# Differential attention on one core: the gate and up products of a feed-forward tile are issued together behind both head pairs' scores, and their tangent one step later

## What is computed

```python
xn = _layernorm(x)
# differential attention: 16 score maps (8 heads x 2), head size 8, causal
scores = jnp.einsum('bhqd,bhkd->bhqk', q, k)
attn = jax.nn.softmax(where(causal, scores, -inf), axis=-1)
attn = attn[:, :, 0] - lam * attn[:, :, 1]
out = jnp.einsum('bhqk,bhkd->bhqd', attn, v)
# feed-forward gate: 4-bit blockwise rounding of inputs and weights
gate = fp4_linear(xn, w_gate)        # 128 -> 352
y = fp4_linear(xn, w_up)             # 128 -> 352
g = _silu(fp4_linear(silu(gate) * y, w_down))   # 352 -> 128
x = x + s * g
```

## Time and profile before

| what | value |
|---|---|
| median of three runs | 691.15 us |
| profiled execution, span | 687.9 us |
| PE matmul busy in the span | 86% |
| ACT busy in the span | 72% |
| DVE busy in the span | 77% |
| one iteration of the middle loop | 40.56 us |

### The profile page before, as it was taken

The page is one execution under the profiler, slowest core; times in us unless marked ns, Lnnn a source line. Parts: engine busy times, 40 slices in busy tenths (PEclk is TensorE's granted clock), DMA queues, the critical chain, the costliest instruction groups (busy, mean ns, idle before and its releaser), DMA issues. The chain is left out here.

```text
span 687.9 us, 15892 instructions
## 1 busy us (share of the span) xinstructions
PE 590.2 (86%) x4825; PEld 355.3 (52%) x4826; DVE 530.8 (77%) x1425; ACT 496.5 (72%) x843; POOL 326.7 (47%) x466
## 2 busy tenths in 40 slices
PE   3576765899999999999999999977999799999960
PEld 2465554233333333333333333375877589999960
DVE  3999998687978889797888877779798856555575
ACT  2367795798989989898998999923455467777741
POOL 0224345344534344452434544252477777776661
PEclk9799998799999999999999999998899979999995
DMA  8000001000544566644466650041122233333475
GB/s 218 16 16 31 20 13 61 1 1 2 102 91 74 82 116 116 115 88 91 63 106 116 116 106 12 1 157 59 59 82 74 80 82 102 95 103 91 131 208 166
DMA packets 76265, 56.06 MB, mean 81 GB/s; under 512 B 6528, under 2 KB 70848, under 8 KB 75968
## 3 DMA queue, kind: packets, MB, share of 16 engines
q1 hardware_dynamic: 70688, 46.01, 30.8%
q0 software_dynamic: 4352, 8.99, 3.9%
q10 hardware_dynamic: 1184, 0.56, 0.3%
HBM read 15.36 MB, written 28.65 MB: 64 GB/s over the span
## 5 line engine op out<-in xcount | busy, mean ns | idle before, releaser
L787 ACT ACTIVATE attend_prob<-attend_ring 128x1024 f32<-128x1024 f32 (+1 forms) x320 | 280.0, 951 | 16.4 <-PE attend_ring L933 14.4
L731 POOL TENSOR_SCALAR_AFFINE_SELECT attend_prob<-attend_prob 128x256 f32<-128x256 f32 x256 | 118.0, 485 | 141.4 <-ACT attend_prob L787 140.8
L953 PE MATMUL attend_ps_o<-attend_prob,attend_v_slot 128*32 128x512 f32 (+3 forms) x1536 | 156.6, 496 | 0.0
L933 PE MATMUL attend_ring<-attend_qk_slot 32*128 32x512 f16 (+3 forms) x672 | 80.1, 329 | 8.1 <-ACT attend_prob L787 6.3
L1907 POOL DMA_INDIRECT expert_outputs<-routed_linear_gated,routed_expert_goal_now x72 | 70.3, 977 | 29.7 <-issue 23.9
L1033 POOL DMA_INDIRECT slots<-rows,slot_index x64 | 62.1, 971 | 37.3 <-issue 33.2
L933 PEld LDWEIGHTS attend_ring<-attend_qk_slot 32*128 32x128 f16 x672 | 22.4, 91 | 106.7 <-ACT attend_prob L787 37.6
L1935 DVE TENSOR_TENSOR outed_linear_head_normed<-outed_linear_head_normed,routed_linear_ps_c 128x256 f32<-128x256 f32 x72 | 30.2, 420 | 41.3 <-ACT outed_linear_head_normed L2029 36.8
L953 PEld LDWEIGHTS attend_ps_o<-attend_prob,attend_v_slot 128*32 128x32 f32 x1536 | 33.7, 108 | 44.9 <-issue 37.7
L2076 PE MATMUL routed_linear_ps_c<-outed_linear_head_normed,head_turned 128*128 128x128 f32 x384 | 52.5, 281 | 1.1 <-ACT head_turned L2010 1.1
L369 POOL TENSOR_TENSOR project_parts_q<-project_rotated_q,project_parts_q 128x1024 f16<-128x1024 f32 x8 | 17.6, 2201 | 68.9 <-ACT project_parts_q L417 68.9
(11 more groups left out here) (291 smaller groups left out, 1281.8 us busy)
## 6 DMA issues: line engine op xcount, KB each, us to landing
slots<-attend_zeros SPq DMA_DIRECT2D x24, 715.0 KB, 10.2
attend_qk_slot<-qk_parts SPq DMA_DIRECT2D x14, 512.0 KB, 3.1
x_pairs<-slots SPq DMA_DIRECT2D x72, 65.0 KB
v_all<-expert_outputs SPq DMA_DIRECT2D x8, 512.0 KB, 5.5
xn_all<-project_xn SPq DMA_DIRECT2D x8, 256.0 KB, 2.3
w<-w_laid SPq DMA_DIRECT2D x1, 2048.0 KB, 7.8
rows<-rows SPq DMA_DIRECT2D x4, 512.0 KB, 3.8
out<-xn_all SPq DMA_DIRECT2D x8, 256.0 KB, 3.5
```

Source lines behind the costliest of these rows:

```text
L731: ins = nc.gpsimd.affine_select(out=edge, in_=edge, compare_op=ALU.is_ge, fill=0.0, base=0, pattern=[[0, 2], [1, P]], channel_multiplier=-1)
L787: nc.scalar.activation(probs(k, pair)[:, :, 0:width], scores[:, :, 0:width], ACT.Exp, scale=HD ** -0.5).then_inc(exp_made[u][pair], 1)
L933: ins = nc.tensor.matmul(dst[:, s * QC + at:s * QC + at + cols], qk[rows, T + j * P:T + (j + 1) * P], qk[rows, qc * QC + off:(qc + 1) * QC ...
L953: ins = nc.tensor.matmul(ps_o[RB * s:RB * (s + 1), off:QC], v4[slot][:, j, s], probs(k, s // 2)[:, s % 2, at:at + cols], start=j == 0, sto ...
```

## The change

In `ORDER` and in PE's queue, the gate product of a tile moves from ahead of its step's scores to behind both pairs' scores, and the up product, which stood between the pairs, follows the gate product directly. The tangent on ACT moves from ahead of the exponentials of step 5i + 3 to behind them (`GATED` = 4). On DVE the two products move by 3 ticks, and the seven parts of the rounding by 3 ticks. Nothing is added or taken out; no shape changes.

```diff
-        GATE, HIDDEN, DOWN, CHUNK = 3, 7, 9, 11
+        GATE, GATED, HIDDEN, DOWN, CHUNK = 3, 4, 7, 9, 11
         PERIOD = STEPS // GT
         ORDER = [("x", 0)]
         for k in range(STEPS):
+            ORDER += [("scores", k, 0), ("scores", k, 1)]
             if k % PERIOD == GATE:
                 ORDER.append(("gate", k // PERIOD))
-            ORDER += [("scores", k, 0), ("scores", k, 1)]
...
-                if (i := at_tile(n, GATE, 0)) is not None:
+                if (i := at_tile(n, GATED, 0)) is not None:
                     act.wait_ge(gate_made, 4 * it + i + 1)
...
-                if (i := at_tile(n, GATE, 2)) is not None:
+                if (i := at_tile(n, GATED, 1)) is not None:
                     dve.wait_ge(th_made, 4 * it + i + 1)
...
-                if (i := at_tile(n, GATE, 3)) is not None:
+                if (i := at_tile(n, GATED, 2)) is not None:
                     dve.wait_ge(u_made, 4 * it + i + 1)
...
-                for part, tick in enumerate((0, 1, 2, 3, 4, 5, 6)):
-                    if (i := at_tile(n, GATE + 1, tick)) is not None:
+                for part, tick in enumerate((3, 4, 5, 6, 7, 8, 9)):
+                    if (i := at_tile(n, GATED, tick)) is not None:
...
                     if tick == 0:
+                        scores(it, k, 0)
+                        scores(it, k, 1)
                         if alone:
                             gate(it, k // PERIOD)
-                        scores(it, k, 0)
-                        if alone:
                             up(it, k // PERIOD)
-                        scores(it, k, 1)
```

## The result

The changed kernel took 695.37 us, the median of five runs (694.81 to 699.28), the kernel before 691.51 us (689.38 to 691.56) on the same chip. The ratio is 1.0081 with a 95% interval of 1.0062 to 1.0101: 0.8% slower. The profiled execution's span is 693.7 us instead of 687.9, **+5.8 us**; its own time is 695.39 us. I take as the end of the attention phase the first ACT row of the next stage, which starts at 461.78 us instead of 455.70; the last DVE row of the phase (the earlier trace rows of before) ends at 460.33 instead of 454.25. Both are +6.08 us, so all of the loss lies in the phase.

What follows compares the result with a forecast made beforehand. The prediction took ACT's stream as the attention phase's clock. Terms 4.8 - 0.7 + 1.9 = +6.0 us took the span from 687.9 to 693.9 us, with 3.25 us more 697.1 us (0.9% slower); 8-in-10 range 688 to 704 us.

Steps and rivals of the forecast that it cites:

- Limit: Attention phase: ACT's stream is the clock; ACT's next wait for PE after a tile becomes 0.5 to 0.8 us.
- Gate and up together, 1.39 us: PE at each tile: the two adjacent products cost 1.39 us instead of 1.58 us, bounds 1.20 and 1.58.
- The added wait: PE at each tile: the gate product now waits for the last exponential ahead of the step's own.
- Kind A: Tiles 1 and 3 (steps 8 and 18): each loses 0.32 us, 15 counted for +4.8 us.
- kind B: Tiles 0 and 2 (steps 3 and 13), short unit ahead of the tile: even, 229.89 against 229.90 us.
- 18.08 + 0.05: Tile 1: exponentials end at 218.08 us and the gate product starts 0.05 us later, at 218.13.
- The first tile, -0.7: Phase start, once: step 3's scores no longer stand behind the gate product; -0.7 us, bounds -1.2 and -0.1.
- The last tile, +1.9: Phase end, once: the tangent comes 1.9 us later and DVE's chain follows; +1.9 us, bounds 1.0 and 2.2.
- DVE's turn, at nothing: Middle loop: DVE's turn of `ps_o` ends just before step 13's values want it; no cost, 0.06 us in hand.
- the rival: DVE becomes late in the loop, its turn coming after PE wants it: 700.6 to 704 us, chance 0.14.
- PE's saving is passed on: Every tile, if the gate product need not wait: up to 16.6 us faster, 674.5 to 683 us, chance 0.15.
- no change: Gate and up products need only 1.20 us, so gains and losses nearly cancel: 691.5 us, chance 0.14.

Runs made afterwards that it cites:

- joined ahead: Kernel before with gate and up products together ahead of both pairs' scores, all else as before: 747.93 us (0.9886), again 750.91 us (0.9906).
- the pair with the short exponential: Kernel before and changed kernel, each with half the columns of unit 7's second-pair exponential left out: 756.51 us (0.9942) and 756.83 us (0.9972).
- Relieving DVE: Two rounding parts and the head sum moved behind DVE's turn: changed kernel 762.68 us (1.0109), products behind the values 756.71 us (0.9982).
- tiles 0 and 2 alone: The change made for tiles 0 and 2 only, tiles 1 and 3 as in the kernel before: 760.55 us, 1.0077 of the kernel before.
- the products behind the values: Changed kernel with gate and up products moved on behind the values of step k - 3: 786.29 us, 1.0406 of the kernel before.

## Why the prediction was right

The forecast was +0.9% (697.1 us), measured was +0.8%; +6.0 us in the phase, measured +6.08. By its steps:

- **Limit.** The place to look is ACT's next wait for PE: 0.63 and 0.73 us, of 0.5 to 0.8 foretold. That ACT's stream is the clock of the whole phase was too broad: at tiles 1 and 3 of the kernel before, 0.43 us less of ACT's work brought nothing, so there PE's own queue set the pace. The stretched pairs shrank from 2.08 and 2.10 to 1.94 us, and the iteration came to 41.39 us, of 41.2.
- **Gate and up together, 1.39 us.** Measured 1.38 us in the changed kernel, from the gate's weight load on, and 1.28 us joined ahead, where that load is under the transpose. The saving was real, and the kernel with the products joined ahead shows what it is worth where no wait eats it.
- **The added wait.** Shown by the pair with the short exponential: 0.85 us of the iteration come and go with the exponential's length, in the changed kernel only.
- **Kind A +0.32 and kind B 0, mis-sized by 0.05 each.** Measured +0.37 and +0.05. The step that was off is the release "18.08 + 0.05": that 0.05 us was read at a load of the scores. In the changed kernel the last exponential ends at 212.52 + 5 x 0.92 + 1.02 = 218.14, by the pace of a row of exponentials, and the gate's load starts at 218.24, 0.10 us later. The loop is 15 x (0.37 + 0.05) = 6.3 us instead of 4.8.
- **The first tile, -0.7, beyond its bound of -1.2.** Measured -1.5. The order of events was right. The exponential of step 4 was forecast for 128.8 us and came at 127.89. Of these 0.91 us, 0.35 are the gate product, which started at 123.84 instead of 124.19 because DVE's chain ahead of it ran as much earlier (its `attend_xq_power` row is at 118.57, before 118.91); 0.12 are the two products, 2.62 us instead of 2.74; and 0.44 are the clock. The sum had taken a middle between full and half clock for the values, and they ran at nearly full clock: 0.81 between 126 and 127 us and 1.00 behind it, while in the kernel before it is 0.50 there and 0.54 between 127 and 128. How much of the earlier clock belongs to the order and how much to chance stays open. The stretch from the first exponential to that of step 4 took 10.92 to 11.86 us in the five profiles in which tile 0 is treated wholly as the change has it, and 12.42 to 13.63 us in the three in which it is wholly as before; the longer ones of either kind are those in which the clock rose later.
- **The last tile, +1.9.** Measured +1.38 from the exponentials of its last six on (435.28 to 455.70 before, 439.98 to 461.78 after). Of it +1.84 is the later tangent, as foretold. The rest is in DVE's chain, 12.52 us instead of 12.98: four roundings took 0.52 us instead of 0.58 to 0.61, 0.33 us in all. These rows show one of them and POOL's masks in the kernel before, then the same rounding in the changed kernel. Before, the roundings run beside POOL's masks; after, POOL's last mask has ended at 450.07, ahead of this rounding.

```profile
443.31 2.33 POOL L731 TENSOR_SCALAR_AFFINE_SELECT attend_prob<-attend_prob 128x256 f32<-128x256 f32 x4 [0.22 <-ACT attend_prob L787]
444.13 0.61 DVE L573 SCALAR_TENSOR_TENSOR attend_hq_power<-attend_hq 128x352 f32<-128x352 f32 x1
```

```profile
450.58 0.52 DVE L573 SCALAR_TENSOR_TENSOR attend_hq_power<-attend_hq 128x352 f32<-128x352 f32 x1
```

- **DVE's turn, at nothing.** Right, and safer than said: it ends at 228.72 and the values come at 229.38, 0.66 us in hand instead of 0.06. Relieving DVE changes nothing. But how near the rival is, two experiments show: with tiles 0 and 2 alone and with the products behind the values it comes true.

```profile
228.02 0.70 DVE L839 STREAM_TRANSPOSE attend_o_t<-attend_ps_o 128x512 f32<-128x512 f32 x1
...
229.38 1.06 PE L953 MATMUL attend_ps_o<-attend_prob,attend_v_slot 128*32 128x512 f32 x8
```

The sum with measured terms: 6.3 - 1.5 + 1.38, and -0.13 for the phase's earlier start, is 6.05 us, of 6.08. The errors in it (+1.5 in the loop, -0.8 and -0.5 at the ends) nearly cancelled; that is luck, and the total is closer than its terms deserve.

The rivals: "PE's saving is passed on" fell at its condition, for the gate product does wait; "no change" fell because gate and up take 1.38 us and not 1.20.

## What to carry to other kernels

In a ring of buffers served in order, a moved piece takes over another predecessor: before counting what PE saves, look who reads the buffer three places back, and when. Products side by side are cheaper (here 0.20 us a tile), and so are the scores that come to stand side by side by it (0.31 us a tile), but the saving arrives only where the joined block's own wait is long over: ahead of the scores it was worth -8.0 us, behind them +6.1 us. And work that moves later on one engine makes another late: behind the values the block was level with the kernel before only after DVE had been relieved. And where two engines take turns as the limit, halving one suspected instruction in both kernels tells which of them waits for it.

## What the runs showed of the hardware that was not expected

- PE's granted clock fell from 0.99 to 0.50 (of 2.4 GHz, so to 1.2 GHz) when PE took up work after 2.17 us of waiting, and was at 1.00 again in the window that starts at 237 us. The kernel with the products behind the values paid twice for this wait: 2.17 us of standing, and some 1.5 us more for the values and the gate product at the lower clock (1.86 and 1.34 us from start to start, instead of 1.00 and 0.69). Its waits of 0.80 us and those of 0.6 us in the changed kernel had no such effect: the clock is 1.00 behind them.
- From the end of an exponential to the start of the weight load that it releases it took 0.10 us for the gate product's load (128 rows, fp32), and 0.05 us for a load of the scores (32 rows, f16).
- Scores of two pairs side by side cost as much on the record as those of one (0.40 to 0.43 us for eight matmuls, 0.39 for four; 0.34 us from start to start, against 0.33). So they gain more by the joining of the products (0.31 us a tile) than the products themselves (0.20 us).
- The same rounding of 128 x 352 on DVE (L570 to L579) takes 0.51 to 0.53 us or 0.58 to 0.69 us at the same line. In the phase of the kernel before, each of the 57 longer ones overlaps an instruction of POOL and none of the 71 shorter ones does. In the changed kernel and in that with the products joined ahead some of the shorter ones overlap one too, so a long rounding goes with POOL's work beside it, but not every rounding beside POOL is long. No run tried it by itself.
